# A Mamba and expert-routing block on one core: the causal mask as zeros in the C-B products with a clamp, two small products on GpSimd, a silu read from its PSUM bank, and a first tap made by ScalarE a step ahead

## What is computed

```python
zxbcdt = h @ Wi                                   # z, xBC, dt
conv = cb + sum(xp[:, k:k + L, :] * cw[:, k] for k in range(4))   # causal, four taps
xs, Bm, Cm = split(silu(conv))
dt = softplus(dt + dtb)
dA = exp(dt * -exp(Alog))
def step(hs, inp):                                # over 512 tokens
    hs = hs * dA_t + dtx_t * B_t
    y = einsum('bhpn,bn->bhp', hs, C_t)
y = rmsnorm((y + D * xs) * silu(z), gw)
h = h + y @ Wo
```

## Time and profile before

| | |
|---|---|
| median of 3 runs | 1203.54 us (1201.79, 1203.54, 1203.59) |
| the profiled execution | 1201.13 us, of which the span is 1199.3 us |
| mean granted TensorE clock | 0.961 of full speed |
| busy: PE, DVE, ACT, POOL | 1056.5, 1001.3, 889.5, 578.0 us |
| the 32 steps with a part A | `hn` of item 0 at 28.4 us, of item 31 at 781.3 us |

### The profile page before, as it was taken

The page is one execution under the profiler, slowest core; times in us unless marked ns, Lnnn a source line. Parts: engine busy times, 40 slices in busy tenths (PEclk is TensorE's granted clock), DMA queues, the critical chain, the costliest instruction groups (busy, mean ns, idle before and its releaser), DMA issues.

```text
span 1199.3 us, 27505 instructions
## 1 busy us (share of the span) xinstructions
PE 1056.5 (88%) x7160; PEld 603.5 (50%) x7160; DVE 1001.3 (83%) x1864; ACT 889.5 (74%) x1724; POOL 578.0 (48%) x721
## 2 busy tenths in 40 slices
PE   5699999999999999999999999997688876999980
PEld 4245544455445554455445554444344444777760
DVE  6798999999998999888998899885578875888865
ACT  5688888888888888888888888886466543565540
POOL 0254566446654566435543455434245451566661
PEclk9899999999999999999999999999789987999995
DMA  4111422233222322210000100000010014776737
GB/s 137 36 34 34 144 91 83 83 115 122 84 85 85 136 98 85 75 29 23 22 22 24 29 19 24 22 16 1 3 33 32 27 36 142 233 227 219 233 117 210
DMA packets 85581, 98.08 MB, mean 82 GB/s; under 512 B 20698, under 2 KB 65888, under 8 KB 85536
## 3 DMA queue, kind: packets, MB, share of 16 engines
q1 hardware_dynamic: 80544, 89.08, 23.5%
q0 software_dynamic: 4992, 8.48, 2.1%
HBM read 59.67 MB, written 37.83 MB: 81 GB/s over the span
## 4 chain that ended last, share of the span: by engine, by line
PE 53%; DVE 20%; issue 13%; ACT 8%; DVEq 2%; DMA 1%; POOL 1%; SPq 1%; ACTq 0%; POOLq 0%
PE bank L475 8%; PE bank L548 5%; ACT xbc L1062 4%; DVE cv L1331 4%; PE bank L604 3%; PE bank L522 3%; PE bank L667 3%; DVE cv L1327 3%; PE bank L484 2%; PE bank L485 2%; PE bank L492 2%; PE bank L491 2%; DVE stmp L1434 2%; DVE M L1341 2%; PE bank L668 2%
## 5 line engine op out<-in xcount | busy, mean ns | idle before, releaser
L1331 DVE SCALAR_TENSOR_TENSOR cv<-bank,PAR,cv 128x511 f32<-128x511 f32 (+2 forms) x384 | 273.8, 740 | 9.1 <-DVE cv L1327 4.2
L1637 POOL TENSOR_TENSOR yt<-yt,ti 128x384 f32<-128x384 f32 x64 | 64.2, 1004 | 331.0 <-DVE ti L1453 331.0
L1341 DVE TENSOR_TENSOR M<-E,bank 128x512 f32<-128x512 f32 x256 | 170.6, 677 | 38.8 <-PE bank L548 30.9
L929 ACT ACTIVATE E<-bank 128x512 f32<-128x512 f32 x256 | 148.6, 594 | 28.1 <-DVE M L1341 27.6
L475 PE MATMUL bank<-hn,WA 128*128 128x512 f32 x256 | 144.6, 647 | 21.0 <-DVE cv L1331 20.6
L1668 POOL DMA_INDIRECT RS<-y,XR x92 | 99.6, 1083 | 78.1 <-DVE y L1546 56.4
L1079 ACT ACTIVATE hr<-bank,W1B 128x512 f32<-128x512 f32 x92 | 63.3, 688 | 57.1 <-PE bank L669 53.4
L1661 POOL DMA_INDIRECT XS<-stage,IDX x64 | 64.5, 1008 | 79.5 <-DVE run L1306 55.7
L1062 ACT ACTIVATE xbc<-cv 128x512 f32<-128x512 f32 x128 | 77.0, 626 | 21.7 <-DVE yt L1448 20.5
L1641 POOL TENSOR_TENSOR y<-yt,zs 128x512 f32<-128x512 f32 x64 | 81.3, 1271 | 20.6 <-POOL yt L1637 19.9
L548 PE MATMUL bank<-M,dtx 128*32 128x128 f32 x2048 | 82.5, 278 | 9.9 <-DVE M L1341 7.3
(11 more groups left out here) (242 smaller groups left out, 2657.5 us busy)
## 6 DMA issues: line engine op xcount, KB each, us to landing
XS<-PADT SPq DMA_DIRECT2D x32, 520.0 KB, 4.0
WA<-w_in SPq DMA_DIRECT2D x192, 64.0 KB, 1.8
W1B<-WD SPq DMA_DIRECT2D x23, 514.0 KB, 3.5
W2B<-WD SPq DMA_DIRECT2D x23, 512.5 KB, 4.9
WD<-WS SPq DMA_DIRECT2D x16, 512.0 KB, 2.7
XR<-XS SPq DMA_DIRECT2D x23, 260.0 KB, 4.4
RW<-w_in SPq DMA_DIRECT2D x18, 256.0 KB, 4.3
WO_raw<-w_out SPq DMA_DIRECT2D x32, 128.0 KB, 3.5
```

Source lines behind the costliest of these rows:

```text
L929: f(E[i % 2][:, :], bank[2 + i % 2][:, :], ACT.Exp).then_inc(e_a, 1)
L1331: stt(out=cv[t][:, s:L], in0=src[:, 0:L - s], scalar=PAR[:, bass.ds(cw + 3 - s, 1)], in1=cv[t][:, s:L], op0=ALU.mult, op1=ALU.add).then_in ...
L1341: tt(M[i % 4][:, :].rearrange("p (n t) -> p n t", n=4), E[i % 2][:, :].rearrange("p (n t) -> p n t", n=4), bank[5][:, c * CH:(c + 1) * CH] ...
```

## The change

The mask is no longer put into the exponents. Four things take its place. `causal`, a 0/1 matrix, is multiplied into the products of C and B in bank 5, in place, once per step (VectorE, new). `apply_decay` becomes a three-operand instruction that takes `min(E, 1)` before it multiplies. The eight spare rows of each 32 of `PC` and `nselb` hold a coarse mask by blocks of 16 tokens, so that exponents far above zero get -1e30 from the product that is made anyway. For that, `PC <- p2` is issued as four DMAs of 24 rows. `dt_` and `wdec` move to GpSimd, `dt_` to the start of its step and `wdec` behind `p2`. The silu of z1 reads bank 1 itself and comes first of the six; z0 keeps its copy and comes third. The first tap of projection 1 is made by ScalarE at the end of the step before (`early_tap`) and no longer by VectorE.

```diff
-SILU_TURN = [3, 4, 0, 5]
+SILU_TURN = [3, 4, 1, 5]
...
 # SyncE
-                    sp.dma_start(PC[:, :], p2[:, :]).then_inc(p4_in, 16)
+                    if not B:
+                        wait(sp, const_v, 10)
+                    for c in range(NC):
+                        q = 32 * c
+                        sp.dma_start(PC[q:q + 24, :], p2[q:q + 24, :]).then_inc(p4_in, 16)
...
 # TensorE, decays(n)
-                        mm(bank[2 + b][:, :].rearrange("p (n t) -> p n t", n=4), idb[:, :],
-                           maskb[:, :].unsqueeze(1).to_broadcast([P, 4, P]), start=True, stop=False)
-                    for b in range(2):
                         q = 32 * (pair + b)
                         mm(bank[2 + b][:, :], PC[q:q + 32, :], nselb[q:q + 32, g * 512:(g + 1) * 512],
-                           start=False, stop=False, tile_position=(q, 0))
+                           start=True, stop=False, tile_position=(q, 0))
...
 # TensorE, before the early projection 1
-                    wait(pe, zc_a, 2 * k + 2)
+                    wait(pe, silu_a, 6 * k + 1)
                     project_early(k + 1, 1)
...
 # ScalarE
+            def early_tap(n):
+                first = act.snap(n // NB * NPAR)
+                wait(act, pj_mm, 6 * n + 2)
+                wait(act, silu_a, 6 * (n - 1) + SILU_TURN[1] + 1)
+                f(cv[1][:, :], bank[1][:, :], ACT.Identity, scale=PAR[:, bass.ds(first + C_CW + 4 + 3, 1)],
+                  bias=PAR[:, bass.ds(first + C_CB + 1, 1)]).then_inc(tap_v[1], 1)
...
-                    wait(act, dtc_v, 4 * k + 1)
+                    wait(act, step_p, 2 * k + 1)
                     f(dA[:, :], dt_[:, :], ACT.Copy, scale=PAR[:, bass.ds(pk + C_NA, 1)]).then_inc(da_a, 1)
...
-                    wait(act, pj_mm, 6 * k + 6)
-                    f(zraw[1][:, :], bank[1][:, :], ACT.Copy).then_inc(zc_a, 1)
...
+                    wait(act, pj_mm, 6 * k + 6)
+                    wait(act, fin_p, 4 * (k - 1))
+                    f(zs[:, bass.ds((k % 2) * 2 * L + L, L)], bank[1][:, :], ACT.Silu).then_inc(silu_a, 1)
                     silu(TB)
...
                     silu(TC)
+                if N:
+                    early_tap(k + 1)
...
 # VectorE
+                def causal_products():
+                    g = bank[5][:, :].rearrange("p (c t) -> p c t", c=NC)
+                    wait(dve, g_mm, j + 1)
+                    tt(g, g, causal[:, :].unsqueeze(1).to_broadcast([P, NC, CH]), ALU.mult).then_inc(g_v, 1)
...
-                    tt(M[i % 4][:, :].rearrange("p (n t) -> p n t", n=4),
-                       E[i % 2][:, :].rearrange("p (n t) -> p n t", n=4),
-                       bank[5][:, c * CH:(c + 1) * CH].unsqueeze(1).to_broadcast([P, 4, CH]),
-                       ALU.mult).then_inc(m_v, 1)
+                    stt(out=M[i % 4][:, :].rearrange("p (n t) -> p n t", n=4),
+                        in0=E[i % 2][:, :].rearrange("p (n t) -> p n t", n=4), scalar=1.0,
+                        in1=bank[5][:, c * CH:(c + 1) * CH].unsqueeze(1).to_broadcast([P, 4, CH]),
+                        op0=ALU.min, op1=ALU.mult).then_inc(m_v, 1)
...
 # GpSimd
+                if A:
+                    wait(pool, dta_a, 5 * k + 3)
+                    wait(pool, tr_mm, k)
+                    tt(dt_[:, :], u[:, :], ln1[:, :], ALU.add).then_inc(step_p, 1)
...
                     tt(p2[:, :], r1[:, :], p1[:, :], ALU.add).then_inc(part_p, 1)
+                    wait(pool, dta_a, 5 * k + 4)
+                    tt(wdec[:, :], dt_[:, :], ecs[:, :], ALU.mult).then_inc(step_p, 1)
```

More of the change, by code:

```diff
@@ L122, in build @@
         xbc = [sb(f"xbc{t}", L) for t in range(4)]
-        zraw = [sb(f"zraw{t}", L) for t in range(2)]
+        zraw = sb("zraw", 2 * L)[:, 0:L]
         u, ax, ex, ln1 = sb("u", P), sb("ax", P), sb("ex", P), sb("ln1", P)
@@ L611, in body @@
                     project(5)
-                    wait(pe, dtc_v, 4 * k + 4)
+                    wait(pe, dtc_v, 2 * k + 2)
+                    wait(pe, step_p, 2 * k + 2)
                     if N:
@@ L659, in _ @@
             project_early(0, 1)
-            pe.wait_ge(const_v, 9)
+            pe.wait_ge(const_v, 10)
             pe.wait_ge(hup, NB)
@@ L1021, in body @@
                     wait(act, pj_mm, 6 * k + 5)
-                    f(zraw[0][:, :], bank[0][:, :], ACT.Copy).then_inc(zc_a, 1)
+                    f(zraw[:, :], bank[0][:, :], ACT.Copy).then_inc(zc_a, 1)
                 if B:
@@ L1062, in silu @@
                         f(xbc[t][:, :], cv[t][:, :], ACT.Silu).then_inc(silu_a, 1)
+                    wait(act, pj_mm, 6 * k + 6)
+                    wait(act, fin_p, 4 * (k - 1))
+                    f(zs[:, bass.ds((k % 2) * 2 * L + L, L)], bank[1][:, :], ACT.Silu).then_inc(silu_a, 1)
                     silu(TB)
-                    for t in range(2):
-                        if t == 0:
-                            wait(act, zc_a, 2 * k + 2)
-                        wait(act, fin_p, 4 * (k - 1))
-                        f(zs[:, bass.ds((k % 2) * 2 * L + t * L, L)], zraw[t][:, :], ACT.Silu).then_inc(silu_a, 1)
+                    wait(act, zc_a, k + 1)
+                    f(zs[:, bass.ds((k % 2) * 2 * L, L)], zraw[:, :], ACT.Silu).then_inc(silu_a, 1)
                     silu(X0)
@@ L1355, in running_sum @@
                     nc.vector.tensor_tensor_scan(cum[:, :], ones_row[:, :], dA[:, :], 0.0, ALU.mult, ALU.add).then_inc(dtc_v, 1)
-                def decay_to_end():
-                    wait(dve, dta_a, 5 * k + 4)
-                    tt(wdec[:, :], dt_[:, :], ecs[:, :], ALU.mult).then_inc(dtc_v, 1)
                 def chunk_decay():
@@ L1376, in body @@
                     tap(0, 1)
-                    tap(1, 0)
                     tap(0, 2)
@@ L1382, in body @@
                 if B:
+                    causal_products()
                     apply_decay(0)
-                if A:
-                    softplus()
                 if B:
@@ L1586, in _ @@
             tt = nc.gpsimd.tensor_tensor
+            for c in range(NC):
+                nc.gpsimd.iota(u[32 * c:32 * c + 32, :], pattern=[[1, 8], [0, 16]], base=24, channel_multiplier=-1,
+                               allow_small_or_imprecise_dtypes=True).then_inc(below_p, 1)
+                pool.wait_ge(below_p, c + 1)
             nc.gpsimd.memset(PADT[:, :], 0.0).then_inc(padt_p, 1)
```

39 lines of the change are left out of this document (20 added, 19 removed).

## The result

The changed kernel took 1210.86 us (median of 4 runs, 1208.07 to 1213.58), the kernel before 1202.85 us in the same comparison: 1.0075 of it, 95% interval 1.0059 to 1.009. The change makes the kernel slower by three quarters of a per cent. The profiled execution took 1208.07 us with a span of 1206.3 and a mean granted clock of 0.951; the other three runs had 0.944 to 0.946.

The account below looks back on a forecast made before the run. No single engine was taken as the bound. Steps 2 to 30 (8.7 us), 31 (0.3) and 32 (0.9) gain, against step 1 (+0.6 - 0.3) and step 0 (+0.3): -9.3 us, forecast 1193 us, range 1184 to 1207.

Parts of the forecast that it names:

- 29 x 0.30: Steps 2 to 30 of the loop: each 0.30 us shorter, 8.7 us in all.
- projection 4 starts 0.12 us later: TensorE in the loop step: projection 4 starts at 405.97 and not 405.85, held by tap 3 of projection 2.
- the 0.54 of the masks: TensorE behind projection 4: `decays(3)` without its pair of mask products is 0.54 us shorter.
- `o_sb` had 404.35 - 404.12 = 0.23 us of slack: VectorE at `o_sb`: 0.23 us of slack behind the output projection, so `o_sb` comes only 0.2 us later.
- released projection 4 by tap 3 of projection 2: TensorE: projection 4 starts at 405.85, when tap 3 of projection 2 has ended at 405.71.
- Rival 4: Clock falls to 0.52, TensorE products take about twice their time: over 1250 us, chance 0.02.
- the last lands 1.9 us later: Four DMA issues of `PC` from SyncE: last load 1.9 us later; step 1 gets +0.6 - 0.3 us.
- The 0.7 us to spare: Loads in the loop: the last `PC` load lands some 0.7 us before `decays(0)` asks for it.
- The early tap: ScalarE, behind the silu of C: `u` and `sqy` 0.7 us later, sum of squares 0.4 later, projection 2 0.3 earlier.
- The mask's product: VectorE ahead of `M` 0: `causal_products` takes 0.61 us plus 0.18 for dependence; each `M` 0.06 more.
- rival 3: Mask product in PSUM becomes VectorE's bound, over 1.1 us, delaying `o_sb`: slower, 1208 to 1218 us, chance 0.15.
- What is hidden: Work off the path: `dt_` and `wdec` on GpSimd cost 0.43 us each, `dA` is not late.

Follow-up runs that it names:

- e9: Changed kernel without the early tap, P4 loads on their own semaphore, VectorE's taps, mask product and `spend` in another order: 1187.01 us.
- e13: e9 with `o_sb` made earlier by moving `M` 3 from ahead of the third tap of xB to behind the fourth: 1194.76 us.
- e2: Changed kernel with the three P4 loads on a semaphore of their own, so `decays(0)` waits only for the PC loads: 1208.05 us.
- e8: Changed kernel with `dt_` and `wdec` put back from GpSimd on VectorE: 1210.21 us.
- e12: e9 with one line moved, `o_sb` ahead of the third tap of xB: 1207.15 us.
- e4: Kernel before with the mask part alone (product, clamp, coarse mask, four PC loads), no moves to GpSimd and no early tap: 1213.92 us.
- e1: Changed kernel with the first tap of projection 1 back on VectorE, so no early tap: 1200.41 us.
- e5: Changed kernel with the early tap in its own buffer behind the silu of z0, and P4 loads on their own semaphore: 1194.37 us.
- e3: Changed kernel with throwaway TensorE products ahead of each pair of exponents in `decays(0)` to `decays(2)`: 1215.22 us.

## Why the prediction was wrong

The forecast was 1193 us and faster; it is 1211 and slower. Against the forecast of -9.3 us the span moved by +7.0: 16.3 us apart. By steps of the sum, in the order of size (the start, at +0.3 for nothing, and the end, at -0.6 for -1.2, make up the rest):

**The sum, 29 x 0.30.** The 26 steps from 145.74 on won 0.08 each at the full clock: 0.22 x 26 = 5.7 us are missing, and 1.3 more in steps 2 to 4. By pieces: first tap to projection 4 took 12.55 us for 12.13, +0.42 where "projection 4 starts 0.12 us later" was forecast; projection 4 to `M` 5 took 3.62 for 4.14, -0.52 where the 0.54 of the masks was forecast; `M` 5 to the next first tap +0.02 where 0.12 was. So one step failed, **"`o_sb` had 404.35 - 404.12 = 0.23 us of slack"**. After the change too, `o_sb` starts 0.23 us behind the end of the output projection (410.45 against 409.20 + 1.02), with VectorE idle for 0.75 us ahead of it. The same 0.23 is the median over the 26 steps in 13 of the 15 kernels, however long VectorE had stood idle; only in e9 (0.61) and e13 (0.26) did its own queue make `o_sb` later. Those 0.23 us are what passes between the two engines, not slack. The output projection was 0.43 us late behind the squares (0.53 late, forecast 0.4), and `o_sb` was 0.43 late with it, where the slack was to leave 0.2. The other part of the miss is the path behind `o_sb`. The prediction released projection 4 by tap 3 of projection 2. This row of the kernel before shows another order:

```profile
405.19 0.64 PE L548 MATMUL bank<-M,dtx 128*32 128x128 f32 x16
```

`within(0)` starts 0.15 us behind the end of `o_sb` (404.35 + 0.69) and projection 4 right behind `within(0)`. From `o_sb` to projection 4 it is 1.50 us before and 1.49 after (411.94 - 410.45). So what is late at `o_sb` is late at projection 4, and the 0.54 that the masks of `decays(2)` gave TensorE ended as its 0.53 of idle time at `within(0)`. e13 shows the other direction: `o_sb` earlier, projection 4 earlier.

**Rival 4, the clock.** 5.5 us in the profiled execution. It had a chance of 0.02, because a thin stretch of the kernel before kept its clock (7.41 of 10 us busy). That compared a mean busy share. What is new is a single wait of 1.05 to 1.18 us in all but one step, and behind it the clock fell in three of 26. Over all kernels, with the longest wait of TensorE in those steps: falls in the changed kernel (1.18), e2 (1.17), e8 (1.06) and once in e12 (0.92); none in e4 (0.98), e9 (0.92), e1 (0.91), e5 (0.78), e3 (0.66) and the rest, all shorter. So a long single wait is what the falls have in common, but between 0.91 and 0.98 its length doesn't sort the kernels, and why it is these steps and not others with the same wait stays open. The Trainium skill ("TensorE: Matmul & The Clock Gate", section "Why this matters for your kernels") warns that idle gaps between bursts take the clock down. The trace agrees in kind, but the page warns of longer gaps than any in these steps, so by itself it doesn't give these falls. The size was wrong in my rival: not 20 us for a step but 2.4 or 0.7, since the clock is back 6.8 or 3.4 us later. That the other runs, with clocks of 0.944 to 0.946, were slower for the same reason is argued and not shown.

**The loads of step 1, "the last lands 1.9 us later", +0.6 - 0.3.** +3.1 instead of +0.3. The four issues of `PC` take 3.23 us where one took 0.57, so the last load is issued some 2.6 us later; `decays(0)` waits for the count of all seven, and TensorE waits 3.35 and not 1.70 us. e2 takes 2.8 back. But e4 waited 3.02 us there and lost nothing, so what the sum lacked is the clock, which fell to 0.5 for 6.8 us behind the wait in the changed kernel, for 3.4 us in e1 and not at all in e4. What decides that, no run shows. The 0.7 us to spare that the prediction gave these loads in the loop weren't there either, but that cost nothing (e2).

**The early tap.** Right in size: `u` 0.66 us later behind the silus (0.7 forecast), a new wait for the squares of 0.58 (0.7 forecast), projection 2 no longer late. Wrong in the balance: I set its lateness against gains of VectorE that e1 shows to be worth less than it. The wait for `u`, 1.16 us long, was in the sum as a part of projection 2's time and nowhere as a wait.

**The mask's product.** 0.69 + 0.21 = 0.90 us from its start to that of `M` 0, where 0.61 + 0.18 = 0.79 was taken. `M` with a third operand takes 0.679 us for 0.677: the clamp is free, I had charged 0.12 behind projection 4. That rival 3 gave the right sign is chance: none of its mechanism was seen. In another surrounding, e4, the same product costs 0.43 a step.

**What is hidden.** `dt_` and `wdec` on GpSimd take 0.45 and 0.46 as forecast and hold nothing there. But they push GpSimd's sum for `h` into VectorE's `spend`, which takes 0.86 to 0.89 us for 0.23 in 13 of the 26 steps; that I had not seen. In the changed kernel it costs nothing: the steps with a `spend` of 0.23 are as long, 24.52, and VectorE waits 0.81 us ahead of `M` 5 in them where it waits 0.15. In e5, where it takes 1.17, the steps with it are 24.43 and those without 24.31.
